# Three elementwise steps on GpSimd, each written as one instruction instead of two or three

## The reference

```python
# layer 0, attention: 16 heads of 128, causal
q, k, v = (einsum('bsd,hed->bhse', x, W) for W in (W_Q, W_K, W_V))
pattern = softmax(where(causal, -1e9, einsum('bhse,bhme->bhsm', q, k) * scale))
out = einsum('bhse,hde->bsd', einsum('bhsm,bhme->bhse', pattern, v), W_O)
# layer 0, feed-forward: 32 experts of width 96, top 6, and a shared part
routed = einsum('tef,efd,te->td', silu(x @ wg) * (x @ wu), wd, combine)
# layer 1, state space: projection, causal convolution of 4 taps, 8 heads, gate, rms norm
M = G * L ; Y = einsum('bclsh,bcshp->bclhp', M, h)      # G = C B^T, L = decays
# layer 1, feed-forward: 16 experts of width 176, top 4 in 2 of 4 groups, and a shared part
out = sum_e cw[:, e] * (swiglu(x @ up[e].T) @ down[e].T) + shared
```

## Time and profile before

| what | value |
| --- | --- |
| median of 3 runs | 1567.08 us (1567.02 to 1567.57) |
| the profiled execution: time, span | 1567.08 us, 1565.3 us |
| granted TensorE clock, mean | 0.992 |
| PE busy | 1487.6 us, 95% |
| DVE busy | 1102.9 us, 70% |
| ACT busy | 744.1 us, 48% |
| POOL busy | 542.7 us, 35%, 531 instructions |

### The profile page before, as it was taken

How to read it: one execution, slowest core, us unless ns; L and a number is a source line. 1 busy time by engine, 2 the same in 40 slices (tenths; PEclk the granted TensorE clock), 3 DMA queues, 4 the chain that set the end, 5 groups by cost and what they waited for, 6 DMA issues and landing times.

```text
span 1565.3 us, 29335 instructions
## 1 busy us (share of the span) xinstructions
PE 1487.6 (95%) x9433; PEld 1306.8 (83%) x9433; DVE 1102.9 (70%) x3031; ACT 744.1 (48%) x1967; POOL 542.7 (35%) x531
## 2 busy tenths in 40 slices
PE   6999999999999989999999999999899799999997
PEld 5989898988989887887888888887688688987886
DVE  5878788787878776555557677867977747532697
ACT  5767666666666544433622353325333544453221
POOL 3323232333323102432358325744682412000650
PEclk9999999999999999999999999999999999999999
DMA  7564655464655105666676557646565789798884
GB/s 266 203 227 176 243 184 214 154 245 154 244 194 195 68 1 155 188 194 182 201 232 201 166 169 220 209 138 209 173 214 169 219 284 300 241 284 257 292 261 143
DMA packets 129738, 315.87 MB, mean 202 GB/s; under 512 B 15968, under 2 KB 39216, under 8 KB 128608
## 3 DMA queue, kind: packets, MB, share of 16 engines
q1 hardware_dynamic: 125024, 301.95, 58.9%
q0 software_dynamic: 4608, 12.59, 2.4%
HBM read 225.35 MB, written 88.60 MB: 201 GB/s over the span
## 4 chain that ended last, share of the span: by engine, by line
PE 48%; issue 20%; POOL 13%; DVE 12%; ACT 6%; DMA 1%; SPq 1%; ACTq 0%; DVEq 0%; POOLq 0%
PE psum L511 41%; POOL act_sb L842 6%; POOL mix L861 4%; POOL xs L874 2%; PE psum L1749 2%; ACT p_sb L976 1%; DVE s_sb L1330 1%; PE psum L1760 1%; ACT kT_hi L935 1%; PE psum L1739 1%; POOL square_sum L866 1%; PE psum L1988 1%; ACT p_sb L974 1%; DVE s_sb L1328 1%; DVE kT_lo L1209 1%
## 5 line engine op out<-in xcount | busy, mean ns | idle before, releaser
L511 PE MATMUL psum<-xT_hi,gu_w 128*128 128x512 f32 x1088 | 373.7, 403 | 12.0 <-DVE act_sb L1380 11.4
L842 POOL TENSOR_TENSOR act_sb<-act_sb,comb 128x512 f32<-128x512 f32 x96 | 158.4, 1651 | 361.1 <-DVE act_sb L1380 360.9
L511 PEld LDWEIGHTS psum<-xT_hi,gu_w 128*128 128x128 f32 x1088 | 206.3, 190 | 63.6 <-DVE act_sb L1380 11.5
L1017 ACT ACTIVATE gated<-psum 128x512 f32<-128x512 f32 (+1 forms) x138 | 82.5, 598 | 371.7 <-PE psum L511 369.4
L795 POOL TENSOR_TENSOR split_stage<-raw_stage,split_stage 128x256 fp32r<-128x256 f32 x168 | 121.0, 748 | 327.7 <-ACT split_stage L925 327.7
L1380 DVE TENSOR_TENSOR act_sb<-psum,gated 128x512 f32<-128x512 f32 (+1 forms) x138 | 95.0, 688 | 177.7 <-PE psum L511 169.5
L511 PE MATMUL psum<-xT_lo,gu_w 128*128 128x512 f32 x544 | 216.0, 397 | 0.0
L511 PEld LDWEIGHTS psum<-d_w,act_hi 128*128 128x128 f32 (+1 forms) x1104 | 149.9, 189 | 13.2 <-issue 1.5
L511 PE MATMUL psum<-d_w,act_hi 128*128 128x256 f32 (+1 forms) x1104 | 154.2, 282 | 0.0
L974 ACT ACTIVATE p_sb<-s_sb,neg_max 128x128 f32<-128x128 f32 x128 | 51.5, 403 | 160.4 <-DVE neg_max L1330 160.3
L511 PEld LDWEIGHTS psum<-xT_lo,gu_w 128*128 128x128 f32 x544 | 103.4, 190 | 18.8
(11 more groups left out here) (257 smaller groups left out, 4013.1 us busy)
## 6 DMA issues: line engine op xcount, KB each, us to landing
gu_w<-w_split SPq DMA_DIRECT2D x138, 512.0 KB, 3.8
w_split<-split_stage SPq DMA_DIRECT2D x56, 768.0 KB, 4.0
d_w<-w_split SPq DMA_DIRECT2D x138, 256.0 KB, 4.1
bw<-l_w SPq DMA_DIRECT2D x63, 496.0 KB, 3.6
xs<-zeros SPq DMA_DIRECT2D x21, 1280.0 KB, 7.3
raw_stage<-w_all SPq DMA_DIRECT2D x56, 384.0 KB, 4.6
decay_all<-decay_dram SPq DMA_DIRECT2D x32, 384.0 KB, 5.3
in_w<-w_split SPq DMA_DIRECT2D x40, 256.0 KB, 4.1
```

Source lines behind the costliest of these rows:

```text
L511: last = nc.tensor.matmul(out_ap, w, m, start=start and n == 0, stop=stop and n == len(pairs) - 1, **kw)
L842: pool.tensor_tensor(act_sb[:, s % 2, :], act_sb[:, s % 2, :], comb[:, comb_block(s) % 2, :], ALU.mult).then_inc(comb_done, 1)
L1017: act.activation(gated[to, s % 2, :], psum[0:to.stop - to.start, G_BANK, :], ACT.Silu).then_inc(gated_ready, 1)
```

## The change

Three functions on POOL are rewritten. Each did its work in two or three instructions on pieces of a tile and told the others after the last; now each does it in one instruction over the whole. The elements, the waits ahead of it and the semaphore behind it are as before.

```diff
@@ low_part
-                for at in range(w.start, w.stop, PART):
-                    w = slice(at, at + PART)
-                    last = pool.tensor_tensor(aw_lo[:, w], aw_raw[:, w], aw_hi[:, w].bitcast(F32), ALU.subtract)
-                last.then_inc(aw_split, 1)
+                pool.tensor_tensor(aw_lo[:, w], aw_raw[:, w], aw_hi[:, w].bitcast(F32), ALU.subtract).then_inc(aw_split, 1)
@@ split_low
-                for j in range(3):
-                    last = pool.tensor_tensor(split_stage[:, k % 2, j, 1, :], raw_stage[:, k % 2, j * PART:(j + 1) * PART],
-                                              split_stage[:, k % 2, j, 0, :].bitcast(F32), ALU.subtract)
-                last.then_inc(split_lo, 1)
+                pool.tensor_tensor(split_stage[:, k % 2, :, 1, :], raw_stage[:, k % 2, :].rearrange("p (j w) -> p j w", j=3),
+                                   split_stage[:, k % 2, :, 0, :].bitcast(F32), ALU.subtract).then_inc(split_lo, 1)
@@ mixes
-                for b in range(2):
-                    last = pool.tensor_tensor(mix[:, g % MIXES, b, :], mix[:, g % MIXES, b, :], gram[:, b, :], ALU.mult)
-                last.then_inc(mix_ready, 1)
+                pool.tensor_tensor(mix[:, g % MIXES], mix[:, g % MIXES], gram[:], ALU.mult).then_inc(mix_ready, 1)
```

## The result

The changed kernel takes 1579.41 us (median of 4 runs, 1578.04 to 1580.86) against 1567.32 for the kernel before (4 runs, 1567.02 to 1567.58): 1.0073 times as long, 95% interval 1.0059 to 1.0086. So it is slower by 10 to 12 us, where 5.8 had been forecast, and the time lies outside the range.

The account below looks back on a forecast made before the run. The prediction took PE to bound nearly all of the kernel. Its terms summed to 1565.3 + 5.9 - 0.1 + 0.0 = 1571.1 us of span, with 1.8 outside it 1572.9 us; range 1566.7 to 1577.0.

Parts of the forecast that it names:

- the turn between instructions: In attention, a DVE scaling gets its turn between two POOL instructions, not inside one.
- the indirect DMAs: Four pairs of mixes behind these, where DVE stands still through the whole pair: merging was to gain 0.6 us.
- Rival 3: An output in three strips costs as much as three instructions, 2.2 us a split: 1577.9 us, chance 0.05.
- The place at 146 us: Attention split at 146.21: DVE's second scaling ends later, and PE's wait at 156.62 grows by 0.52 us a group.
- The place at 99 us: Attention split at 99.23: DVE's next instruction starts late, and PE's 0.83 us wait for k's low part grows by 0.32.
- Rival 1: Nobody waits for the longer POOL instructions, so both attention terms vanish: 1566.9 us, chance 0.22.
- The other four splits: In each attention group, four of eight splits end no later than the scaling's usual point: nothing waits, cost zero.
- the low parts: Merged low parts of attention weights: after the first pair, the other 29 end 0.15 us earlier, effect zero.
- the attention term of 5.9: Cost of merged splits in attention: 7 x (0.52 + 0.32) = +5.9 us.
- The start: At the start PE waits for the first pair of low parts, which comes 0.1 us earlier: -0.1 us.
- The mixes: 32 merged mixes: -0.6 us behind indirect DMAs, +0.7 where DVE's scan ran between halves; together 0.
- rival 2: The mixes decide as well, each of seven scans waiting 0.84 us longer: +2.5 on top, 1575.4 us, chance 0.11.

Follow-up runs that it names:

- e9: The changed kernel with DVE's two scalings of p_sb also writing the sum of what they scaled: 1568.07 us, ratio 1.0010.
- e1: The kernel before with only the three pieces of each split merged, low parts and mixes left in two pieces: 1572.88 us, ratio 1.0037.
- e4: The changed kernel with one low part per group, the one directly after the sixth split, kept in two pieces: 1574.88 us, ratio 1.0055.
- e12: The changed kernel with the sixth split of each group kept in three pieces, all low parts merged: 1574.42 us, ratio 1.0047.
- e2: The kernel before with only the two pieces of each low part merged: 1565.96 us, ratio 1.0001; PE's first score product at 22.80 us, 22.69 before.
- e3: The kernel before with only the two pieces of each mix merged: 1569.06 us, ratio 1.0002, interval 0.9991 to 1.0013.
- e6: The changed kernel with p_sb padded and its scalings widened to 129 and 259 columns; the intended one-at-a-time form did not appear: 1580.20 us, ratio 1.0082.
- e11: The changed kernel with the first, sixth and seventh splits kept in three pieces and the low part after the sixth in two: 1568.25 us, ratio 1.0010.
- e7: The kernel before with p_sb padded and its scalings widened to 129 and 259 columns: 1567.19 us, ratio 0.9997.
- e5: The changed kernel run again without any edit: 1578.71 us, ratio 1.0068.
- e10: The kernel before with DVE's two scalings of p_sb also writing the sum of what they scaled: 1567.12 us, ratio 1.0004.

## Why the prediction was wrong, point by point

- **What bounds the kernel, and the turn between instructions: right.** The rule that DVE's scaling gets in only between two POOL instructions explains every wait found in attention; behind the indirect DMAs it doesn't hold, as the prediction says. By the Trainium skill, "SBUF — State Buffer", section "Who interferes with whom", a tensor_scalar contends in its two-port form but not in the form that also writes its accumulator. e9 agrees: its two scalings average 0.347 and 0.476 us, with splits of 1.84 beside them, and in the changed kernel they take up to 1.56 and 1.40.
- **Lengths: right.** 1.839 and 1.283 us, forecast 1.84 and 1.30. Rival 3 is out.
- **The place at 146 us: right.** Forecast 0.52 a group, measured 0.50; PE's wait 0.26 to 0.64 (forecast about 0.8; the rest shows as shorter gaps).
- **The place at 99 us: right in size, not in place.** Forecast 0.32, measured 0.30. But PE's wait for k's low part stayed at 0.82 (forecast 1.15): the delay shows earlier, 0.15 at the transposes of 101.86 and the rest by the score product at 104.01 us (103.31 before). Rival 1 is out.
- **The other four splits, "there DVE is 0.1 us early and nothing waits for it", and the low parts, "zero": this is the step that failed.** Each was costed against the other in its old form. The sixth split was one of the four where the first scaling is near the end; with the low part of 512 columns behind it without a gap, the second scaling falls 0.06 us behind that one's start. Measured 0.70 a group: 0.12 to 0.16 of it with merged splits alone (e1), 0.58 only with both (72.85 - 72.27; e4 takes it away from one side, e12 from the other). 7 x 0.70 = 4.9 us is what the attention term of 5.9 lacked: it measured 7 x 1.50 = 10.5.
- **The start: forecast -0.1.** No run shows it; see e2.
- **The mixes: forecast 0, measured +0.4.** These are differences at PE between the same matmuls of two profiles, so they hold for single executions. The gain behind indirect DMAs is there, and a little larger than forecast (0.8 for 0.6): 0.4 at the pair of 1011.5 us of the kernel before, where PE's wait falls from 1.66 to 1.24, and 0.4 at the other three, between the ticks that begin at 1088.57 and 1131.96, where its wait of 2.34 is 2.17. So the reading of the trace that the prediction put against the rule held: by the rule these four would have cost 3.2. The cost where DVE's scan ran between the halves was forecast at 0.84 for each scan and is 3.39 - 2.56 = 0.83 for the pair of rows 13 (scan: 2.56 before), but between 1131.96 and 1166.11 it comes to +1.05 at PE, with 0.1 more at 850 to 900 us, where the forecast had 0.7 in all. The place at 1011 us, before and changed:
```profile
1014.96 0.47 PE L511 MATMUL psum<-xT_hi,gu_w 128*128 128x512 f32 x1 [1.66 <-DVE act_sb L1380]
...
1022.49 0.47 PE L511 MATMUL psum<-xT_hi,gu_w 128*128 128x512 f32 x1 [1.24 <-DVE act_sb L1372]
```
  And the other two, in the changed kernel (PE; then POOL, DVE and PE at the later pair):
```profile
1116.36 0.50 PE L511 MATMUL psum<-xT_hi,gu_w 128*128 128x512 f32 x1 [2.17 <-DVE act_sb L1372]
...
1141.58 2.28 POOL L854 TENSOR_TENSOR mix<-mix,gram 128x768 f32<-128x768 f32 x1
...
1142.09 3.39 DVE L1541 TENSOR_TENSOR_SCAN mix<-decay_all,start_row 128x768 f32<-128x768 f32 x1
...
1145.40 0.66 DVE L1372 TENSOR_TENSOR act_sb<-psum,gated 128x512 f32<-128x512 f32 x1
...
1146.12 0.50 PE L511 MATMUL psum<-xT_hi,gu_w 128*128 128x512 f32 x1 [0.17 <-DVE act_sb L1372]
```
  The same -0.4, -0.4 and +1.05 are in all eight kernels with merged mixes (the changed one, e3 to e6, e9, e11 and e12) and in none of the five other kernels with mixes in halves. It is too small for a median to show, and far from rival 2's 2.5.
- **A microsecond that the forecast did not have.** In the same eight profiles the granted clock comes back from its lower level later at about 1250 us of the kernel before, and PE loses 1.1 to 1.3 us between 1225 and 1257; with mixes in halves one profile of five loses 0.8 there (e7), the others nothing. The kernel before, then the changed one at the same work:
```profile
1251.00:1253.00 2.00, 2.00 (x17) 1.92 (x16) 0.59 (x2) 1.29 (x5) 0.00 (x0) 1.00 0.25 86
...
1260.00:1262.00 2.00, 2.00 (x12) 2.00 (x11) 0.58 (x2) 0.93 (x3) 0.00 (x0) 0.50 0.30 95
```
  How the mixes would do this was not tested, so it is not shown that they do. With the mixes it would make 1.5 us, still within e3's interval.
- **The sum with the measured terms:** 1572.9 + (10.5 - 5.9) + 0.4 = 1577.9, and 1579.0 with the microsecond of clock, against 1579.4 and 1578.7. The profiled execution was 3.7 us below the median of four. Part of that was luck: between 1257.27 and 1453.38 us of its span it took 196.1 us, and the same program in e5 took 200.5 for the same work. What sets that stretch from one execution to the next stays open; the kernel before scatters as well (1564.2 to 1570.8 in 23 runs). The forecast of an unchanged time behind 604 us can't be judged within its 1 us for this reason.

No version beat the kernel before. e9, e10 and e11 equal it within 0.1%; e10's period is shorter by 0.1 to 0.2 us, which is about 1 us in all and below what the runs tell apart.

## What to carry to other kernels

When two engines share an access that is given up only at the end of an instruction, cutting an instruction in pieces costs the fixed 0.2 us each (here) and buys the other engine its turns; merging is free only where the other engine has no instruction there or isn't waited for. Two edits on the same engine must be costed together wherever their instructions stand in a row: shift every start of the waiting engine by the new lengths and see behind which instruction it now falls, since missing a turn by 0.06 us costs the whole next instruction. Where the order can't be changed, changing the form of the waiting instruction takes the contention away altogether (e9).

## What the runs showed of the hardware that was not expected

- A scaling that also writes its sum isn't held up by POOL at all, though it is the slower form (0.347 and 0.476 us against 0.29 and 0.34).
- DVE's scan, which reads two buffers in SBUF, is held up in the same way: 1.75 us alone, 3.39 beside a 768-column mix, which itself took 2.28 in place of 1.84.
- A move of the granted clock in one place was larger than some terms of the change. In the kernel before it fell to the lower level (1.2 GHz) for some 3 us at 602 us of the span; at the same place of the program the changed kernel stayed at the upper one (2.4 GHz), and its first expert step took 27.5 us in place of 29.1. Windows of the kernel before (the ten us ahead, and the fall):
```profile
592.40:602.40 10.00, 7.80 (x48) 6.31 (x46) 7.30 (x28) 5.69 (x9) 0.00 (x0) 1.00 0.26 79
...
602.00:606.00 4.00, 3.44 (x9) 2.76 (x10) 2.81 (x10) 0.50 (x1) 0.00 (x0) 0.57 0.46 74
```
  and of the changed one (the same ten us, 9.3 later, and 35 us around them):
```profile
601.70:611.70 10.00, 7.76 (x48) 6.32 (x46) 7.32 (x28) 5.70 (x10) 0.00 (x0) 1.00 0.24 79
...
599.00:634.00 35.00, 32.61 (x196) 27.94 (x195) 24.28 (x71) 13.70 (x25) 7.75 (x12) 1.00 0.52 173
```
  PE had done the same work ahead (7.80 and 7.76 us busy of ten), and the clock fell in one execution and not in the other. What decides it wasn't found. In the account of the span it gives back 1.5 of the changed kernel's loss. With 1.1 from an earlier start and 0.4 for the mixes, this is how that profile comes to 8.2 us where attention alone lost 10.5; what it lost besides to lower clocks near 1030 and 1250 us (1.0 and 1.2) it gained back in the blocks behind (2.1).
